# A macaron block in float32: the first pair's operands and V products made inside the first feed-forward half

## The reference, cut to what matters

```
x = x + 0.5 * ffn(layernorm(x))          # ffn: (silu(x wg^T) * (x wu^T)) wd^T, integer weights / 127
x = x + attention(layernorm(x))          # q, k, v, rope on q and k, causal softmax, output projection
x = x + 0.5 * ffn(layernorm(x))
```

## Time and profile before

| What | us |
|---|---|
| Median of 3 executions (lowest, highest) | 1305.59 (1303.64, 1308.99) |
| The profiled execution's own time | 1308.21 |
| Its span, first to last instruction | 1306.5 |
| PE busy in the span | 1234.4 (94%) |
| ACT busy | 891.0 (68%) |
| DVE busy | 751.8 (58%) |
| POOL busy | 405.2 (31%) |

### The profile page before, as it was taken

One profiled execution on the slowest core, in us unless ns is written; L12 is line 12 of the kernel. 1 busy time (PEld: TensorE's weight loads), 2 busy tenths in 40 slices (PEclk: granted clock), 3 DMA queues, 4 the chain that ended last, 5 costly groups with the idle time before them and its releaser, 6 DMA issues. The chain is left out here.

```text
span 1306.5 us, 26548 instructions
## 1 busy us (share of the span) xinstructions
PE 1234.4 (94%) x7264; PEld 845.3 (65%) x7264; DVE 751.8 (58%) x1789; ACT 891.0 (68%) x1946; POOL 405.2 (31%) x224
## 2 busy tenths in 40 slices
PE   5986599999999999999999999999999999999898
PEld 2543466666676676767676767676767676766465
DVE  5574456665566666565656565556565656554354
ACT  2664377777777777777777777777777777777474
POOL 5132443333333333333333333333333333330000
PEclk9998799999999999999999999999999999999899
DMA  7122455555555555464646464555555545442000
GB/s 275 49 96 74 127 137 136 139 143 131 154 132 137 141 129 157 117 165 118 163 123 163 123 163 123 156 129 155 124 143 131 152 124 156 122 113 55 9 33 32
DMA packets 118462, 164.84 MB, mean 126 GB/s; under 512 B 14368, under 2 KB 64416, under 8 KB 118304
## 3 DMA queue, kind: packets, MB, share of 16 engines
q1 hardware_dynamic: 118032, 163.70, 46.9%
q10 hardware_dynamic: 400, 0.79, 0.3%
HBM read 53.02 MB, written 10.75 MB: 49 GB/s over the span
## 5 line engine op out<-in xcount | busy, mean ns | idle before, releaser
L937 DVE CUSTOM_DVE_ANT_0 probs<-wide,tri_mask 128x1024 f32<-128x1024 f32 (+7 forms) x512 | 383.4, 755 | 417.8 <-PE wide L641 413.5
L822 ACT ACTIVATE probs<-probs,neg_max 128x1024 f32<-128x1024 f32 (+7 forms) x512 | 395.2, 774 | 159.3 <-DVE neg_max L937 155.6
L833 ACT ACTIVATE shared_a<-bank 128x512 f32<-128x512 f32 (+2 forms) x640 | 341.3, 547 | 121.8 <-PE bank L657 118.5
L657 PE MATMUL bank<-ident,probs 128*128 128x128 f32 x2304 | 369.8, 279 | 12.5 <-ACT shared_a L833 10.3
L657 PEld LDWEIGHTS bank<-ident,probs 128*128 128x128 f32 x2304 | 264.8, 140 | 166.7 <-issue 107.7
L92 POOL TENSOR_TENSOR rotated<-terms,cross 128x1024 f32<-128x1024 f32 x62 | 147.6, 2381 | 625.0 <-DVE cross L86 625.0
L640 PE MATMUL wide<-k_hh,q_hl 128*128 128x512 f32 (+3 forms) x768 | 290.6, 381 | 8.4 <-DMA k_hh<-parts 3.5
L674 PE MATMUL bank<-shared_a,v_cur 128*64 128x256 f32 (+3 forms) x1792 | 297.3, 453 | 0.0
L641 PE MATMUL wide<-k_low,q_hl 128*128 128x512 f32 (+3 forms) x768 | 255.9, 343 | 0.0
L674 PEld LDWEIGHTS bank<-shared_a,v_cur 128*64 128x64 f32 x1792 | 108.6, 136 | 119.4 <-issue 72.3
L640 PEld LDWEIGHTS wide<-k_hh,q_hl 128*128 128x128 f32 x768 | 145.6, 190 | 22.5 <-issue 8.4
(11 more groups left out here) (114 smaller groups left out, 1210.2 us busy)
## 6 DMA issues: line engine op xcount, KB each, us to landing
q_hl<-parts SPq DMA_DIRECT2D x254, 128.0 KB, 2.8
k_hh<-parts SPq DMA_DIRECT2D x254, 128.0 KB, 2.7
v_cur<-shared_b SPq DMA_DIRECT2D x32, 512.0 KB, 4.2
inv_sum<-inv_scratch SPq DMA_DIRECT2D x128, 128.0 KB, 3.1
k_low<-parts SPq DMA_DIRECT2D x63, 256.0 KB, 4.1
xn_cur<-xn_scratch SPq DMA_DIRECT2D x15, 1024.0 KB, 6.3
w_qk<-w_scratch SPq DMA_DIRECT2D x32, 256.0 KB, 3.2
w_scratch<-first_w_parts SPq DMA_DIRECT2D x8, 512.0 KB, 3.1
```

What stands on the lines that cost most here:

```text
L657: last = nc.tensor.transpose(ring[at % 2][:, col:col + P], probs[g][:, h, OFFSET[g][r] + j * P:OFFSET[g][r] + (j + 1) * P], ident[:])
L822: nc.scalar.activation(own, own, ACT.Exp, bias=neg_max[g][:, col], scale=-1.0, accum_out=sums[g][:, col]).then_inc(probs_done, 1)
L833: nc.scalar.activation(turned[:, slot, to], ring[at % 2][:, 0:w * len(heads)], ACT.Copy).then_inc(ring_free[at % 2], signals)
L937: nc.vector.tensor_tensor_reduce(out=part_of_probs(g, k), in0=wide_banks[k % 2][:, x0:x1], in1=tri_mask[:, SEQ - (x1 - x0):], scale=1.0, s ...
```

## The change

Pair 0 is finished inside the first feed-forward half, in its last stretch, and so are the V products of the first sequence.

- PE: after `variance_b(6)` V unit 0, then `mean_b(7)`, V units 1 and 3, `variance_b(7)`, V unit 2, into the four banks of gate and up.
- ACT: after chunk 6's root it keeps V unit 0, rounds half 1, squares chunk 7, keeps V units 1 and 3, takes chunk 7's root, keeps V unit 2, and issues its five fills.
- DVE: the sum of half 1 moves behind chunk 7's update of x.
- POOL: each of chunks 4 and 5 is followed by its `low_half`.
- SP: chunk 4's store, eight fills of half 0, the load of pair 1's weights, chunk 5's store, one `fill_low` and four `fill_qk` of half 1, then the stores of chunks 6 and 7.
- Attention: PE begins with pair 1's projection units 0 and 1 (in other banks), then scores 0 and 1, projection units 2 to 5, scores 2 to 7. DVE has pair 1's rope steps 0 to 2, maxima 0 and 1, rope steps 3 to 5, maxima 2 to 7. SP starts with the copy of `v_stage` to `v_cur`. PE's wait for `zeros_done` stands behind the eighth score.

The diff, cut to its core:

```diff
@@ macaron_half, PE
+def first_v(k):
+    project_v_unit(nc, (*gate, *up)[k], FIRST_V[k], ahead.w_v, ahead.xn_cur).then_inc(o.proj_full, 1)
...
 if norm_b:
     variance_b(N_CHUNKS - 2)
+    pe.wait_ge(ahead.v_loaded, 16)
+    pe.wait_ge(silu_done, K * N_CHUNKS)
+    pe.wait_ge(hidden_done, K * N_CHUNKS)
+    first_v(0)
     mean_b(N_CHUNKS - 1, N_CHUNKS)
+    first_v(1)
+    first_v(2)
     variance_b(N_CHUNKS - 1)
+    first_v(3)
@@ ACT
+def keep_first_v(k):
+    act.wait_ge(o.proj_full, 6 + k + 1)
+    if k == 0:
+        act.wait_ge(low_done, N_CHUNKS)
+    if k == 3:
+        act.wait_ge(var_b_full, N_CHUNKS)
+    nc.scalar.activation(mem_b[:, FIRST_V[k], :], (*gate, *up)[k][:], ACT.Copy).then_inc(first_v_kept, 1)
...
     rstd_of_b(N_CHUNKS - 2)
+    keep_first_v(0)
+    act.wait_ge(o.sum_done, 2)
+    round_half(nc, o, 1)
     square_of_b(N_CHUNKS - 1, 1)
+    keep_first_v(1)
+    keep_first_v(2)
     rstd_of_b(N_CHUNKS - 1)
+    keep_first_v(3)
+    act.wait_ge(o.low_done, 2)
+    fill_low(act, o, 0, 1)
+    fill_qk(act, o, 0, 1, 1)
@@ DVE
     nc.vector.scalar_tensor_tensor(out=x[:, cols(c)], in0=down[:], ...).then_inc(x_done, 1)
+    if norm_b and last and u == 1:
+        sum_first(1)
@@ POOL
+def last_body(i):
+    for u in range(2):
+        xn_parts_of_b(pool, nc.gpsimd, 2 * i + u, u, 16 * i)
+        pool.wait_ge(o.high_done, u + 1)
+        settle(pool)
+        low_half(nc, o, u)
-for_each(pool, PAIRS_OF_CHUNKS - 1, body)
-pool.wait_ge(o.high_done, 1)
-low_half(nc, o, 0)
+for_each(pool, PAIRS_OF_CHUNKS - 2, body)
+last_body(PAIRS_OF_CHUNKS - 2)
@@ SP
+store_xn(PAIRS_OF_CHUNKS - 2, 0)
 sp.wait_ge(o.low_done, 1)
 for h in range(2):
     fill_qk(sp, o, 0, 0, h)
 sp.wait_ge(o.proj_full, 6)
 sp.dma_start(ahead.w_qk[:]...)
+store_xn(PAIRS_OF_CHUNKS - 2, 1)
+sp.wait_ge(o.low_done, 2)
+fill_low(sp, o, 0, 0)
+fill_qk(sp, o, 0, 1, 0)
 body(PAIRS_OF_CHUNKS - 1)
@@ attention, PE
+project(0, 1, 0, ahead=True)
+project(0, 1, 1, ahead=True)
+score(0, 0, 0, 0, 0)
+score(0, 0, 0, 0, 1)
+project(0, 1, 2, ahead=True)
...
+project(0, 1, 5, ahead=True)
+score(0, 0, 0, 0, 2)
...
+score(0, 0, 0, 0, 7)
 pe.wait_ge(zeros_done, 4)
-for n in range(2):
-    project_v(0, n, ahead=True)
...
-pe.wait_ge(proj_free, proj_unit(0, 1, 5))
-pe.wait_ge(first_v_kept, 4)
```

More of the change, by code:

```diff
@@ L71, in project_unit, with project_v_unit @@
     return nc.tensor.matmul(out[:, 0:w], w_qk[:, 1, half], xn_cur[:, 0, xs], start=False, stop=True)
+def project_v_unit(nc, bank, n, w_v, xn_cur):
+    for b in range(2):
+        out, keys = bank[:, 256 * b:256 * (b + 1)], slice((2 * n + b) * P, (2 * n + b + 1) * P)
+        nc.tensor.matmul(out, xn_cur[:, 0, keys], w_v[:, 0, :], start=True, stop=False)
+        nc.tensor.matmul(out, xn_cur[:, 0, keys], w_v[:, 1, :], start=False, stop=False)
+        last = nc.tensor.matmul(out, xn_cur[:, 1, keys], w_v[:, 0, :], start=False, stop=True)
+    return last
 def rope_unit(nc, dve, o, bank, n, halves, freed):
@@ L562, in attention @@
         inv_spread = [sem(f"inv_spread{g}") for g in range(2)]
-        AHEAD_UNITS = [(0, n) for n in range(6)] + [(None, 0), (None, 1), (1, 0), (1, 1), (None, 2), (None, 3)] + [
-            (1, n) for n in range(2, 6)]
+        AHEAD_UNITS = [(0, n) for n in range(6)] + [(None, n) for n in range(4)] + [(1, n) for n in range(6)]
         def ahead_unit(u, n):
@@ L609, in project, with project_v @@
                     pe.wait_ge(proj_free, n + 5)
-                project_unit(nc, ring[n % 2] if ahead else proj_bank, n, w_qk, xn_cur).then_inc(proj_full, 1)
-            def project_v(quad, n, ahead=False):
+                project_unit(nc, (out_bank, proj_bank)[n % 2] if ahead else proj_bank, n, w_qk, xn_cur).then_inc(proj_full, 1)
+            def project_v(quad, n):
                 if n == 0:
                     pe.wait_ge(v_loaded, 16 * (quad + 1))
[L615 to L625, removed]
+                pe.wait_ge(proj_free, v_unit(quad, n) - 1)
+                project_v_unit(nc, proj_bank, n, w_v, xn_cur).then_inc(proj_full, 1)
             def score(p, i, u, g, k):
@@ L772, in pair @@
                 ahead_v(3)
-            pe.wait_ge(zeros_done, 4)
-            for n in range(2):
-                project_v(0, n, ahead=True)
[L777 to L787, removed]
-            pe.wait_ge(proj_free, proj_unit(0, 1, 5))
-            pe.wait_ge(first_v_kept, 4)
+            project(0, 1, 0, ahead=True)
[3 more added lines that the diff above has]
+            project(0, 1, 2, ahead=True)
+            project(0, 1, 3, ahead=True)
+            project(0, 1, 4, ahead=True)
+            project(0, 1, 5, ahead=True)
+            score(0, 0, 0, 0, 2)
+            score(0, 0, 0, 0, 3)
+            score(0, 0, 0, 0, 4)
+            score(0, 0, 0, 0, 5)
+            score(0, 0, 0, 0, 6)
+            score(0, 0, 0, 0, 7)
+            pe.wait_ge(zeros_done, 4)
             for u in range(2):
@@ L902, in pair @@
                 ahead_v(3)
[L904 to L912, removed]
             for k in range(7):
@@ L1006, in _ @@
                 nc.vector.memset(inv[g][:], 0.0)
[L1007 to L1014, removed]
+            rope(0, 1, 0, ahead=True)
+            rope(0, 1, 1, ahead=True)
+            rope(0, 1, 2, ahead=True)
+            max_of(0, 0, 0)
+            max_of(0, 0, 1)
+            rope(0, 1, 3, ahead=True)
+            rope(0, 1, 4, ahead=True)
+            rope(0, 1, 5, ahead=True)
+            max_of(0, 0, 2)
+            max_of(0, 0, 3)
+            max_of(0, 0, 4)
+            max_of(0, 0, 5)
+            max_of(0, 0, 6)
+            max_of(0, 0, 7)
             for u in range(2):
```

46 lines of the change are left out of this document (21 added, 25 removed).

## The result

The changed kernel takes 1296.6 us (median of 8; 1294.52 to 1302.24), the kernel before 1308.76 on the same chips (median of 8; its first three runs had 1305.59). The ratio is 0.9925, interval 0.9907 to 0.9942: 9.8 us faster (7.6 to 12.2). The two medians themselves lie 12.2 us apart, at the edge of that interval; beside the later runs the kernel before had medians of 1305.7 to 1308.4, so I go by the ratio. Forecast was a gain of 12.5, to 1293.1, range 1288 to 1299.5.

A forecast was written before the change was run, and what follows sets the result against it. PE was taken as busy 94% of the span, the gain lying in its waits at the seam between first feed-forward half and attention; 16.3 - 4.2 + 1.0 - 0.6 = 12.5 us, to 1293.1, range 1288 to 1299.5.

The forecast's parts named there:

- The update of x and the sum: Tail: x updated at 117.3 instead of 123.78, sum done by 119.3 or 119.9, while PE does chunk 7's mean.
- PE and ACT in the tail: Tail: V products and copies between norm steps; last copy ends 125.4, ACT's last fill issued at 128.4, ACT done at 129.0.
- The seam: Between feed-forward block and attention: ACT ends the block at 129.0, plus 0.7 us, so attention starts at 129.7 instead of 134.81.
- The first score: Start of attention: waits for the last fill, comes at 133.4 instead of 149.66, 16.3 us earlier.
- for fills alone: Last fills before the first score: some 7.5 us from 125.4, to 133.0, if no stores get between.
- late-fills rival: Stores and v_cur crowd the last fills: first score at 136.4, gain 9.5 us, time 1296; chance 0.16.
- the score nearer to 135: If SP's stores share the DMA engines with ACT's last fills, first score nearer to 135, gain 1.5 us smaller.
- From the first score to the loop: First score to end of exponential 7: +16.9 at half clock, +15.0 at high, +16.0 taken against 11.8; 4.2 us given back.
- Pair 0: First hand-over in the loop: wait for pair 1's k_low goes, 1.0 us gained; loop start at half clock costs 0.6.
- The sum: Whole kernel: 16.3 - 4.2 + 1.0 - 0.6 = 12.5 us gained, median 1293.1.
- Given back in the loop: Rival: waits for k_low at 31 hand-overs cost 6 to 12.5 us, time within 0.5% of before; chance 0.08.
- The rule on the shared port: Tail: two-input DVE sum and POOL's SBUF reads exclude each other; sum takes 1.91 us, or everything behind comes 1.2 later.

The follow-up runs named there:

- x_first: Kernel before, with only DVE's sum of half 1 moved behind the update of x and POOL's low_half(0) moved ahead of chunk 5's split; ratio 0.9946.
- late_stores: Changed kernel with SP's stores of chunks 6 and 7 issued in attention, behind the copy of V and load of wo; one execution, 1291.37 us.
- hold_all: Changed kernel with SP's copy of V, load of wo and stores of chunks 6 and 7 issued only after the first score; one execution, 1297.40 us.
- warm: Changed kernel plus 32 matmuls of unused result behind the tail's last V product and 12 before pair 1's projection unit 5; one execution, 1291.95 us.
- old_order: Changed kernel with the order before the change for projections, scores, rope and maxima; ratio 0.9897, 1292.97 us.
- split_hold: Changed kernel with SP's copy, load and stores after the first score, and pair 0's k_low filled by halves, half 0 early; one execution, 1296.57 us.

## Why the prediction held, point by point

- *The update of x and the sum*: right. Mean of chunk 7 at 118.8 (119.2 forecast). `x_first` shows this step alone is worth 5.4 us.
- *PE and ACT in the tail*: the chain was right, and ran 0.4 to 0.7 us ahead of its forecast (ACT's last copy ended at 124.7, not 125.4). That the last fill was issued at 128.8 (128.4 forecast) is luck: the first one went out 1.6 us earlier than forecast, since it did not wait for ACT's root and copy, and the five took 5.1 us from first to last issue instead of 3.0.
- *The seam*: 129.7 forecast, 132.2 measured. I took ACT as the end, and SP's issues at 0.6 us each. SP's last fill was issued 1.7 us later than forecast and its stores took 1.2 us more, so SP ended the block; the 0.7 us for the seam itself came out (131.5 to 132.2). It cost nothing: `late_stores` gave the 2 us back and the first score stayed.
- *The first score*: 133.4 forecast, 134.3 measured; on the common scale the gain is 15.1, not 16.3. My 133.0 "for fills alone" was the right term, 1.5 us too small: alone they hold the score to +17.6, which is 134.5 on the old timeline. The miss would have been larger without the early start: from the first issue to the last landing `hold_all` took 10.4 us, not 7.5. The DMA engines were 0.77 busy in that time, 8.0 us of work: the 7.5 us were near their work and not near the time that it took. The reason of the late-fills rival, and of the score nearer to 135 (stores and `v_cur` among the fills), was wrong: `hold_all` took them away for nothing.
- *From the first score to the loop*: +16.0 forecast, +16.7 and +16.4 measured, near the half-clock end of my range; `warm`, at the high clock, takes 14.7, where I had 15.0. The order is the cause, with the clock that it brings: `old_order` takes 11.7. That is what was given back.
- *Pair 0*: the 1.0 us wait for `k_low` is gone, as forecast (no such wait before 185 us in the changed kernel), but the cold start of the loop ate it: between exponential 7 and the second reciprocal the changed kernel takes 21.2 and 21.1 us, before 21.2. I had +0.4; `warm` takes 20.0. The cold clock was sized at 0.6 and is 1.1.
- *The sum*: 12.5 forecast, 10.5 at the second reciprocal, 9.8 timed. The three terms above, 1.2 + 0.5 + 0.3, make up the 2 us. The steps behind them were to take the middle of the clock's bounds, although the row on PE's pauses spoke for the cold end, and to count the fills of two queues as if they kept the DMA engines full. The forecast 1293.1 also started from a median of 1305.6 for the kernel before, which measured 1308.8 in the comparison; the gain is the fairer test.
- *Given back in the loop*: not as a rule. Thirteen profiles of kernels with a changed head have 0.7 to 4.5 us of waits for `k_low`, the kernel before 2.3; the same kernel had 4.5 and 0.8. From the second reciprocal to the loop's end the 14 profiles take 1032.2 to 1037.9 us, and less these waits 1031.1 to 1033.4, the kernel before 1032.2: no part of the gain went there. The waits scatter by about 2 us to either side, and the second half by 4; together they are as large as the 7.7 us between the fastest and the slowest of the changed kernel's eight runs, which no profile takes apart.
- *The rule on the shared port* (the Trainium skill, "SBUF — State Buffer", section "Who interferes with whom") cost little where I weighed it: DVE's sum, with two SBUF inputs, took 1.40 us, not 1.9. A larger case came from another sentence of that section, that a cast can run in a mode which takes the pair of ports shared with GpSimd, and that the one that issues second is then blocked. The trace agrees: DVE's cast of chunk 6, with one input, took 2.38 us instead of 0.43, started at 121.63 behind POOL's low part (121.28) and done 0.3 us after it, at 124.0. It hid behind the fills.

What stays open: why two `k_low` fills issued at the same moment on two queues stretch the next issues to 1.5 to 2.1 us. That fewer bytes shorten them was shown, the mechanism was not. Nor is it known why the last fill takes 5.1 to 5.7 us from its issue in all of these kernels.

## What to carry to other kernels

Look first at what stands in an engine's program between an input that is ready and the operation that a long chain waits for: here two operations that changed places gave half of the gain by positions, and all the other moves the other half. When work is moved out of a prologue, keep the interleaving of what is left: the new order cost 4.3 us of the 15 that had been won at the first score. Here PE paid 2.4 to 3.0 us for two pauses ahead of its work, so price such work at the low clock unless a row shows otherwise; matmuls of unused result in the pauses won that time back.

## What the runs showed of the hardware that I had not expected

- SP's eight fills on one queue were issued in 0.6 us each in the kernel before. When SP and ACT filled at once and each began with 256 KB into 64 partitions, four of the ten issues took 1.5 to 2.1 us (the changed kernel, `hold_all`); with 128 KB each, 0.6 to 1.3 (`split_hold`).
- The last of those fills landed 5.3 us after its issue in `hold_all`, with nothing but fills in flight (median of such fills over the kernel before: 2.7; its counterpart there, on ACT's queue at 146.21: 3.4).
- ACT's first fill was issued at 123.76 right behind the low part, while its root ran until 124.22 and its copy, ahead of the fill in the program, began at 124.12: the issue waited for neither.
- In the changed kernel PE's granted clock was still 1.0 in the 3 us of idleness from 139 to 142 and 0.50 from 143.5 on, through 10 us in which PE was 89% busy.
